# The start of attention reordered image by image, and the query and key stacks laid out in every sixth partition

## The reference, cut to what matters

```python
def _ln_t(v, eps=1e-05):                       # per token, over 256 channels
    m = jnp.mean(v, axis=-1, keepdims=True); s = jnp.var(v, axis=-1, keepdims=True)
    return (v - m) / jnp.sqrt(s + eps)
t = t + attn2(_ln_t(t)); t = t + ffn2(_ln_t(t)); t = t + attn3(_ln_t(t)); t = t + ffn3(_ln_t(t))
# attention, 16 heads of 16 dims (attn3 with a causal mask)
q, k, v = jnp.split(x @ w_qkv, 3, axis=-1)
attn = softmax(q k^T * SCALE); out = (attn v) @ w_proj + b_proj
# ffn: router over 8 experts on the normalised tokens, the 2 best, their outputs weighted
```

## Time and profile before

| | |
|---|---|
| median of 3 runs (lowest, highest) | 1030.7 us (1028.92, 1030.9) |
| the profiled execution's own time, its span | 1029.4 us, 1027.6 us |
| PE, DVE, ACT, POOL busy | 80%, 44%, 29%, 23% of the span |
| mean granted clock of TensorE | 0.878 |
| attention of layer 2, of layer 3 (first instruction of the block) | from 268.96 us, from 584.12 us |
| router of layer 2, of layer 3 | from 396.57 us, from 706.86 us |

### The profile page before, as it was taken

One profiled execution on the slowest core, in us unless ns is written; L12 is line 12 of the kernel. 1 busy time (PEld: TensorE's weight loads), 2 busy tenths in 40 slices (PEclk: granted clock), 3 DMA queues, 4 the chain that ended last, 5 costly groups with the idle time before them and its releaser, 6 DMA issues. The chain is left out here.

```text
span 1027.6 us, 12446 instructions
## 1 busy us (share of the span) xinstructions
PE 823.8 (80%) x3900; PEld 520.7 (51%) x3901; DVE 447.6 (44%) x1129; ACT 295.5 (29%) x446; POOL 233.5 (23%) x314
## 2 busy tenths in 40 slices
PE   3769379899677786399999187775399999999993
PEld 2758236435544454166666144554256666666662
DVE  4974631698656543522222546554511212121213
ACT  3223135532234562022121133453012121212121
POOL 1150000573201100234443112340211221122110
PEclk8579678999888997599999688898599999999997
DMA  3000070000135602033111425952103006600003
GB/s 109 1 1 1 1 256 1 0 1 0 48 97 167 150 22 90 16 102 108 41 46 41 145 72 157 240 150 72 34 16 144 21 26 270 265 20 26 26 15 133
DMA packets 53617, 80.35 MB, mean 78 GB/s; under 512 B 10020, under 2 KB 45988, under 8 KB 50372
## 3 DMA queue, kind: packets, MB, share of 16 engines
q1 hardware_dynamic: 48040, 67.37, 20.9%
q0 software_dynamic: 5536, 12.46, 4.0%
HBM read 55.82 MB, written 11.27 MB: 65 GB/s over the span
## 5 line engine op out<-in xcount | busy, mean ns | idle before, releaser
L2030 PE MATMUL psum<-ring,f_x_t 128*128 x552 | 254.3, 604 | 1.3 <-DVE f_x_t L1898 1.3
L1891 DVE TENSOR_TENSOR f_gated<-f_silu,psum 128x512 f32<-128x512 f32 x69 | 47.4, 688 | 271.2 <-PE psum L2030 271.2
L2030 PEld LDWEIGHTS psum<-ring,f_x_t 128*128 128x128 f32 x552 | 101.6, 194 | 104.5 <-issue 104.4
L2044 PE MATMUL psum<-ring,f_gated_t 128*128 x552 | 130.7, 380 | 1.8 <-ACT f_gated_t L1957 1.8
L2044 PEld LDWEIGHTS psum<-ring,f_gated_t 128*128 128x128 f32 x552 | 101.2, 190 | 23.4 <-issue 12.7
L1957 ACT ACTIVATE f_gated_t<-psum 128x512 f32<-128x512 f32 x69 | 41.2, 597 | 237.1 <-PE psum L2037 237.1
L1953 ACT ACTIVATE f_silu<-psum 128x512 f32<-128x512 f32 x69 | 41.2, 597 | 113.7 <-PE psum L2030 113.7
L1478 PE MATMUL psum<-a_stack_k,a_stack_q 96*128 96x256 bf16 (+1 forms) x256 | 45.3, 289 | 25.3 <-DMA a_stack_k<-a_parts 14.2
L1758 POOL COPY f_from_now<-f_from_row 128x1 uint32 (+1 forms) x48 | 9.0, 188 | 206.8 <-PE psum L2023 203.3
L1761 POOL DMA_INDIRECT f_xs<-rows_in,f_from_now x48 | 47.5, 989 | 36.5 <-POOL f_from_now L1758 36.5
L1770 POOL DMA_INDIRECT rows_out<-f_y,f_to_now x46 | 46.1, 1001 | 36.4 <-POOL f_to_now L1767 35.3
(11 more groups left out here) (294 smaller groups left out, 1208.1 us busy)
## 6 DMA issues: line engine op xcount, KB each, us to landing
ring<-in_f_experts SPq DMA_DIRECT2D x24, 1536.0 KB, 7.7
a_stack_q<-a_parts SPq DMA_DIRECT2D x96, 64.0 KB, 2.8
a_stack_k<-a_parts SPq DMA_DIRECT2D x96, 64.0 KB, 2.7
rows_in<-h SPq DMA_DIRECT2D x4, 1024.0 KB, 5.8
ring<-rows_out SPq DMA_DIRECT2D x8, 512.0 KB, 5.4
a_wqkv<-in_a_wqkv SPq DMA_DIRECT2D x2, 768.0 KB, 4.4
x_in<-in_x SPq DMA_DIRECT2D x1, 1024.0 KB, 5.5
out<-x SPq DMA_DIRECT2D x4, 256.0 KB, 2.1
```

What stands on the lines that cost most here:

```text
L1891: dve.tensor_tensor(gated[:, b, :], silu[:, b, :], psum[:, 2 * b + 1, :], ALU.mult).then_inc(s_g, 1)
L2030: last = pe.matmul(psum[:, 2 * b + side, :], x_t[:, xb, t, :], k.ring[:, bass.ds(at + start, CHUNK)], start=(t == 0), stop=(t == CT - 1))
L2044: last = pe.matmul(psum[:, Y_BANK, 0:C], gated_t[:, b, P * a:P * a + P], k.ring[:, bass.ds(at + start, C)], start=(c == 0 and a == 0), sto ...
```

## The change

Four things change. Nothing of the arithmetic does.

1. `LayerNorm` works by images: statistics, variance, square root and reciprocal for two tiles at a time, in `image_by_image`, in all four places where it is used. ScalarE still runs `deviation` ahead of all else in its list.
2. In attention the pieces of the projection are 512 tokens (two images) of one half of the channels: 8 pieces (`SPLITS`) of 4 passes, each split into its parts 512 elements wide. Pieces 0 to 3 are images 0 and 1. ScalarE copies out all four turned images (L1402). Five pieces are projected ahead of the first scores (`SPLITS_BEFORE`), three between them (`SPLITS_AFTER`), and the values of the last tiles later than before (`VALUES_AFTER`).
3. The first four groups are loaded group by group, 12 DMAs and a semaphore each.
4. A pair of parts `c` lies in partitions c, c+6, c+12, ... of the stacks, where it lay in 16 partitions in a row. Queries and keys agree in it.

```diff
-    def statistics(self, dve, t):
-        for T in range(TT):
+    def statistics(self, dve, t, i):
+        for T in (2 * i, 2 * i + 1):
             dve.bn_stats(self.raw[:, T, :], t[:, T, :]).then_inc(self.s_raw, 1)
...
     def deviation(self, act):
-        act.wait_ge(self.s_moments, 2)
-        act.activation(self.sd[:], self.var[:], ACT.Sqrt).then_inc(self.s_sd, 1)
+        for i in range(TT // 2):
+            act.wait_ge(self.s_moments, 2 * i + 2)
+            act.activation(self.sd[:, 2 * i:2 * i + 2], self.var[:, 2 * i:2 * i + 2], ACT.Sqrt).then_inc(self.s_sd, 1)
...
+    def image_by_image(self, dve, t, out):
+        self.statistics(dve, t, 0)
+        for i in range(TT // 2):
+            if i + 1 < TT // 2:
+                self.statistics(dve, t, i + 1)
+            self.normalise(dve, t, out, i)
...
-VALUES_AFTER = (1, 4, GROUP, GROUP + 2)
+VALUES_AFTER = (GROUP - 2, GROUP - 1, GROUP, GROUP + 2)
+SPLITS = 2 * 2 * CT
+SPLITS_BEFORE = SPLITS // 2 + 1
+SPLITS_AFTER = (0, 2, 4)
+def split_bank(i):
+    return i if i < SPLITS // 2 else 2 + i % 2
...
-                        sp.dma_start(stack[HD * c:HD * c + HD, g % SLOTS_G],
+                        sp.dma_start(stack[c:STACK:len(COMBOS), g % SLOTS_G],
...
+            for g in range(SLOTS_G):
+                b, t = image_and_half(g)
+                for which in range(2):
+                    for part, done in enumerate((s_hi, s_mid, s_lo)):
+                        sp.wait_ge(done, 2 * t + which + 1)
+                        for c, combo in enumerate(COMBOS):
+                            if combo[which] == part:
+                                sp.dma_start((stack_q, stack_k)[which][c:STACK:len(COMBOS), g],
+                                             parts[:, t, which, part, N * b:N * b + N]).then_inc(s_first[g], 16)
...
+            for i in range(SPLITS_BEFORE):
+                take_rest(i)
+                take_low(i)
...
             for i in range(FIRST_MAXIMA):
                 take_max(i)
+                if i in SPLITS_AFTER:
+                    take_rest(SPLITS_BEFORE + SPLITS_AFTER.index(i))
+                if i - 1 in SPLITS_AFTER:
+                    take_low(SPLITS_BEFORE + SPLITS_AFTER.index(i - 1))
```

More of the change, by code:

```diff
@@ L1183, in attention @@
         s_ht = sm("h_transposed")
[L1184 removed]
+        s_hto = sm("h_t_out")
         s_qk = sm("qk_projected")
@@ L1191, in attention @@
         s_vo = sm("v_out")
-        s_first = [sm("stacks_of_first_heads"), sm("stacks_of_last_heads")]
+        s_first = [sm(f"first_stacks_{i}") for i in range(SLOTS_G)]
         s_st = [sm(f"stack_loaded_{i}") for i in range(SLOTS_G)]
@@ L1216, in attention, with part_of @@
         QUADS = GROUP // 4
+        def part_of(i, part):
+            half, t, which = i // (2 * CT), i // 2 % CT, i % 2
+            return parts[:, t, which, part, BANK * half:BANK * half + BANK]
         def exponentials(i):
@@ L1238, in load_stacks @@
                     for c, combo in enumerate(COMBOS):
-                        sp.dma_start(stack[HD * c:HD * c + HD, g % SLOTS_G],
+                        sp.dma_start(stack[c:STACK:len(COMBOS), g % SLOTS_G],
                                      parts[:, half, which, combo[which], N * b:N * b + N]).then_inc(s_st[g % SLOTS_G], 16)
[L1242 to L1250, removed]
+            for g in range(SLOTS_G):
[7 more added lines that the diff above has]
+                                             parts[:, t, which, part, N * b:N * b + N]).then_inc(s_first[g], 16)
+            sp.wait_ge(s_lo, SPLITS)
             for g in range(GROUPS - 1):
@@ L1292, in _, with take_rest, take_low @@
         def _(dve):
[L1293 to L1302, removed]
+            ln.image_by_image(dve, k.t, normed)
+            def take_rest(i):
                 dve.wait_ge(s_hi, i + 1)
[L1304 removed]
+                dve.tensor_tensor(rest[:, i % 2, 0:BANK], psum[:, split_bank(i), :], part_of(i, 0), ALU.subtract).then_inc(s_r, 1)
+            def take_low(i):
                 dve.wait_ge(s_mid, i + 1)
[L1306 to L1307 removed]
+                dve.tensor_tensor(part_of(i, 2), rest[:, i % 2, 0:BANK], part_of(i, 1), ALU.subtract).then_inc(s_lo, 1)
+            for i in range(SPLITS_BEFORE):
+                take_rest(i)
+                take_low(i)
             def take_max(i):
@@ L1385, in take_values @@
                                psum[:, 4 + i, :].rearrange("p (a h d) -> p a h d", a=2, h=AH), ACT.Copy).then_inc(s_vo, 1)
-            for i in range(TT // 2 - 1):
-                take_values(i)
+            take_turned(0)
+            take_turned(1)
+            split(0)
+            split(1)
+            take_turned(2)
+            take_turned(3)
+            split(2)
+            split(3)
+            take_values(0)
+            take_values(1)
+            for i in range(SPLITS // 2, SPLITS):
+                split(i)
             def negate(g):
@@ L1405, in _ @@
             negate(0)
-            take_values(TT // 2 - 1)
+            for i in range(TT // 4, TT // 2):
+                take_values(i)
             for g in range(GROUPS):
@@ L1425, in _, with turn_image @@
         def _(pe):
-            for i in range(TT // 2):
+            def turn_image(i):
                 pe.wait_ge(ln.s_out, 2 * i + 2)
@@ L1455, in project_values @@
                     last.then_inc(s_v, 1)
+            turn_image(0)
+            turn_image(1)
+            pe.wait_ge(s_w, 16 * WEIGHTS)
+            pe.wait_ge(s_hto, 2)
+            project_part(0)
+            project_part(1)
+            turn_image(2)
+            turn_image(3)
+            project_part(2)
+            project_part(3)
             for T in range(TT // 2):
                 project_values(T)
-            pe.wait_ge(s_r, 2 * CT)
+            pe.wait_ge(s_hto, 4)
+            for i in range(SPLITS // 2, SPLITS_BEFORE):
+                project_part(i)
+            pe.wait_ge(s_r, 2)
             free_of_maxima = (-1, 0)
```

58 lines of the change are left out of this document (27 added, 31 removed).

## The result

| | before | after |
|---|---|---|
| median (lowest to highest, 7 runs each) | 1030.7 us (1026.15 to 1037.16) | 1023.44 us (1021.97 to 1025.24) |
| ratio of the times, 95% interval | | 0.9925 (0.9904 to 0.9946) |
| span of the profiled execution | 1027.6 us | 1021.7 us |
| mean granted clock of TensorE | 0.879 | 0.875 |

The change makes the kernel 0.5 to 1.0% faster. The forecast was 1023.0. That it came within half a us is in part luck: stage by stage the sum was off in both directions, and the experiments found that most of the change is not needed for its gain.

What follows compares the result with a forecast made beforehand. Bound: a serial chain at attention's start (LayerNorm and projection, SP's stack DMAs, first maxima), TensorE idling, then at half clock. Terms -6.7 - 4.9 + 4.0 = -7.6 us took 1029.4 to 1021.8, as a median 1023; range 1016 to 1029.

Steps and rivals of the forecast that it cites:

- LayerNorm and the first piece: Start of attention: first projection +7.5 us after the block's start, against +8.27; first stack DMA near +11.7 in layer 2.
- TensorE becomes the link: Before attention's first scores: TensorE's own work, not the stacks (+21.8), sets their start at +23.1, against stacks at +31.5 before.
- VectorE next: First maxima: VectorE sets the pace; main loop at +40.9 in layer 2 (gain 6.7 us), +39.4 in layer 3 (4.9).
- the clock falls between the scores: Rival, 4%: at half clock the first-scores stage costs about 10 us more per layer, one partial fall 2.
- The routers: Both routers: later LayerNorm and a missing rise of TensorE's clock lose 2.0 us each, 4.0 us for two.
- the case that no rise comes: Routers: TensorE's clock doesn't rise at all, and each router loses 2.9 us.
- The main loop is the same instructions: Attention's main loops: SP's first ring transfer comes 1 to 3 us into the loop, hidden by 8 units.
- 0.645, nothing gained: Stack DMAs to every sixth partition: SP's issue sets the pace and stays 0.645 us each; bounds 0.43 and 0.645 + 0.2.
- the stacks become cheap: Rival, 10%: issues fall towards 0.43 us; main-loop waits shrink by at most 3.9 us, giving 1019.
- half the gain in attention: Rival, 12%: hand-overs between engines cost 0.3 us more at 14 steps; gains only 3 and 2 us, giving 1029.5.
- The sum: Whole kernel: -6.7 and -4.9 in attention, +4.0 in routers, -7.6 us in all; median 1023.

Runs made afterwards that it cites:

- experiment 10: The whole change, with ScalarE's roots of images 2 and 3 placed behind the copies of images 0 and 1; 1021.29 us, 0.9910 of the kernel before.
- Experiment 3: The whole change, with TensorE repeating the four transposes of images 0 and 1 into unused banks in the routers' gaps; 1017.28 us, 0.9883 of the kernel before.
- experiment 1: The kernel before with one part alone: the first four groups loaded group by group, a semaphore each; 1018.29 us, 0.9897.
- experiment 6: The kernel before with group-by-group loads and stacks in every sixth partition, one queue, nothing else; 1015.73 us, 0.9861.
- experiment 8: The kernel before with group-by-group loads, group 1's issued by GpSimd beside SP's, and stacks in every sixth partition; 1008.69 us, 0.9752.
- experiment 9: The whole change, with the old LayerNorm of all images at once in both attentions and both routers; 1019.52 us, 0.9900 of the kernel before.
- experiment 11: The whole change, with routers' LayerNorm all at once and attention's roots of images 2 and 3 behind the copies of 0 and 1; 1016.03 us, 0.9833.
- experiment 7: The kernel before with group-by-group loads, group 1's 12 issued by GpSimd beside SP's 36, stacks in consecutive partitions; 1028.93 us, 1.0001.

## Why the prediction held, step by step

**LayerNorm and the first piece: right.** The first projection was put at +7.5 and came at +7.54 because of the roots ahead of the copies; experiment 10 moved them and it came 0.5 earlier. The first DMA was put at +11.7 and came at +11.95 and, in layer 3, at +11.64.

**"TensorE becomes the link": right.** First scores +23.2 (forecast +23.1) with no wait, first maximum +26.03 (+26.0). In layer 3 the first maximum was at +24.85.

**"VectorE next": right, 1 us short.** The eighth maximum ended at +35.4 (forecast +35.6), the main loop came at +41.94 against +40.9. The missing 1 us is the clock, which I had expected to stay full: the stretch 305.7 to 309.1 shows it at 0.51 while the last value tiles and scores ran. Experiment 3, whose attention is the same code, happened to keep its full clock there, and its main loop started at +40.80, as forecast (307.14, its block beginning at 266.34):

```profile
303.00:308.00 5.00, 3.62 (x24) 2.77 (x24) 2.68 (x5) 2.67 (x4) 1.28 (x2) 1.00 0.39 96
...
307.14 0.60 PE L1554 MATMUL psum<-a_stack_q,a_stack_k 98*128 98x256 bf16 x4 [1.31 <-DMA a_stack_q<-a_negated]
```

That is the rival "the clock falls between the scores", given 4%, come true in its smallest form. In layer 3 the forecast was +39.4, and +38.71 came. Gains: -5.7 for -6.7, -5.6 for -4.9; together -11.3 for -11.6.

**The routers: right in kind, too cheap.** 2.0 us each were forecast, 2.7 and 2.9 came, near the 2.9 that the prediction gave for the case that no rise comes. I had taken off 0.9 for a rise of the clock during the logits that did not come; experiment 3 brought it by filling.

**"The main loop is the same instructions", so no change: wrong in layer 3**, by +3.2 us. TensorE was busy there for 62.16 us in place of 59.71, at 0.85 in place of 0.91, while its waits for stacks and rows of maxima went from 4.8 to 5.3 us: most of it is the clock. The loop starts 5.3 us before SP's last load is issued, and experiments 1, 6 and 8 show that such a loop can lose time: 82.2 to 82.8 us with the loads late, 78.8 and 78.9 with them early. For the whole change itself the late loads don't decide it. Experiments 9 and 11 have the same loads, the last issued 3.9 and 4.4 us into layer 3's loop, and take 79.2 and 79.3 us for it, at a clock of 0.91. What set the clock in one and not in the other is open.

**The stride, "0.645, nothing gained": right about the issue, wrong about the time.** The issue stayed at 599 ns. But I had looked for the price of a transfer in its issue alone, and the landing fell by 0.5 to 0.7 us at the same issue. On the kernel before the stride was worth 0.6 to 1.1%, of which the waits explain a part; within the whole change nothing that can be measured (0.9925 with, 0.9948 without). And I had set aside the limit of the layout because a DMA share of 0.37 seemed to speak against it. It didn't: one queue issues 64 KB in 0.645 us, 102 GB/s, and two queues got no more than 100 to 123 through the old layout. The issue and the layout bound the pace at about the same value, so a low share hid the second limit, and only a second queue (experiments 7 and 8) showed it. The rival "the stacks become cheap" had the mechanism half right, the time not: it expected a shorter issue. (A slip in another rival: for half the gain in attention its own terms give 1029.7, not 1029.5.)

**The sum:** -5.9 in the span for -7.6. Against the forecast the starts of attention gained 0.3 us less, the routers lost 1.6 more and the main loops, put at nothing, lost 2.0; the experts' stages, which the change doesn't touch, gave 2.1 back, for no cause that the traces name. The medians differ by 7.3, since the profiled execution before was 1.3 under its median, and the one after was its median. So the mechanism at the start of attention and in the routers was right, and the closeness of 1023.44 to 1023 is luck in part.

What I had not asked at all is which part of the change carries it. Loads by group alone give 1.0%, the stride alone 0.8%, LayerNorm by images costs 5 to 6 us in the routers and gives nothing measurable in attention, and projections by 512 tokens, with the last value tiles behind them, bring the scores forward by 2.9 and 3.5 us and put the main loop back by 3.6 and 2.1 through VectorE.

## What to carry to other kernels

Make a consumer wait for the smallest set of transfers that it needs, in the order in which it needs them, before cutting the work ahead into smaller pieces: a cut piece that comes earlier must not push its remainder in between the next stage's instructions on the engine that bounds it. When SP's issue pace and the bandwidth of a layout lie close together, neither a second queue nor a spread layout shows its worth alone (0.9897 by itself, 1.0001 with two queues, 0.9861 with the spread, 0.9752 with both); try them together. Where TensorE waits under 1 us between bursts ahead of a serial chain, compare with useless work in the gap.

## What the hardware showed that I had not expected

- With one queue, 64 KB spread over every sixth partition land 0.5 to 0.7 us sooner at the same issue time: 2.0 to 2.1 us against 2.6 to 2.8 in 16 neighbouring partitions.
- Two queues, each of whose transfers writes 16 neighbouring partitions, moved 100 to 123 GB/s together at a DMA share of 1.13 to 1.26, and the median transfer landed after 4.6 to 8.3 us; with the spread, up to 183 GB/s at a share of 0.68. A high share with few GB/s was the sign of it.
- GpSimd took 0.53 us for one of its DMA issues (0.53 and five in 2.75), no slower than SP.
- Eight extra transposes of 128x128 in two gaps of 0.81 us took the following 32 small matmuls from 6.97 to 5.05 us, by the clock.
- The same 582 matmul records of a main loop kept TensorE busy for 59.7 us at a granted clock of 0.91 and for 62.2 at 0.85 in layer 3, for 64.9 at 0.98 and 68.1 at 0.92 in layer 2.
